# Another order of the score, maximum and value matmuls in an attention step of a fused adaLN block

## The reference, cut to what matters

```python
scores = jnp.einsum('bhqd,bhkd->bhqk', q, k) * scale
scores = jnp.where(causal_mask, -jnp.inf, scores)
attn = jax.nn.softmax(scores, axis=-1)
out = jnp.einsum('bhqk,bhkd->bhqd', attn, v)
```

## Time and profile before

| what | us |
|---|---|
| median of 3 runs | 3058.89 (3057.62 to 3067.77) |
| span of the profiled execution | 3061.1 |
| PE busy | 2843.4 (93%) |
| DVE busy | 2242.9 (73%) |
| ACT busy | 1779.3 (58%) |
| POOL busy | 1253.7 (41%) |
| first to last exponential of attention | 343.1 to 2122.4 |

### The profile page before, as it was taken

One profiled execution on the slowest core, in us unless ns is written; L12 is line 12 of the kernel. 1 busy time (PEld: TensorE's weight loads), 2 busy tenths in 40 slices (PEclk: granted clock), 3 DMA queues, 4 the chain that ended last, 5 costly groups with the idle time before them and its releaser, 6 DMA issues.

```text
span 3061.1 us, 61038 instructions
## 1 busy us (share of the span) xinstructions
PE 2843.4 (93%) x22500; PEld 1573.9 (51%) x22500; DVE 2242.9 (73%) x5047; ACT 1779.3 (58%) x2736; POOL 1253.7 (41%) x1557
## 2 busy tenths in 40 slices
PE   7888799999999999989999999987999999999997
PEld 4433333333433334433333333323888999999997
DVE  7888788888888888899998888822393225566477
ACT  2422466666566665656665566665556666666533
POOL 6766311213521114521114765554305753443176
PEclk9999899999999999999999999998999999999998
DMA  4854323313312322412323535245336765665486
GB/s 163 209 142 106 110 56 65 66 42 76 101 39 56 66 63 59 109 43 37 66 63 91 141 94 123 89 129 152 117 93 204 233 202 175 187 183 173 136 238 193
DMA packets 290690, 359.05 MB, mean 117 GB/s; under 512 B 65404, under 2 KB 243212, under 8 KB 290140
## 3 DMA queue, kind: packets, MB, share of 16 engines
q1 hardware_dynamic: 259516, 279.94, 33.8%
q0 software_dynamic: 26112, 71.34, 7.7%
q10 hardware_dynamic: 4768, 3.88, 0.5%
HBM read 206.25 MB, written 139.21 MB: 113 GB/s over the span
## 4 chain that ended last, share of the span: by engine, by line
PE 49%; ACT 13%; DVE 10%; POOL 7%; issue 7%; DMA 2%; ACTq 1%; POOLq 0%; SPq 0%; DVEq 0%
ACT P L1643 13%; PE PB L1165 10%; PE PB L1092 8%; PE PB L1181 7%; DVE mx L1460 6%; PE PB L1062 6%; PE PB L1039 6%; PE PB L1075 5%; POOL x_slots L1846 4%; PE PB L1106 2%; PE PB L1150 2%; ACTq L1652 1%; POOL yg L1859 1%; PE PB L1129 1%; POOL x_slots L1838 1%
## 5 line engine op out<-in xcount | busy, mean ns | idle before, releaser
L1460 DVE TENSOR_REDUCE mx<-PB 128x1 f32<-128x512 f32 (+3 forms) x2560 | 1406.9, 603 | 214.6 <-PE PB L1039 135.6
L1643 ACT ACTIVATE P<-PB 128x1024 f32<-128x1024 f32 (+3 forms) x1280 | 1095.4, 894 | 643.3 <-PE PB L1075 629.3
L1039 PE MATMUL PB<-KO,QO 64*128 64x512 bf16 (+3 forms) x2560 | 762.0, 353 | 61.5 <-DVE mx L1460 51.5
L1092 PE MATMUL PB<-P,V 128*17 128x512 f32 (+3 forms) x5120 | 599.2, 540 | 11.8 <-POOL P L1797 11.7
L1062 PE MATMUL PB<-QO,KO 64*128 64x512 bf16 (+3 forms) x2560 | 546.8, 353 | 60.0 <-ACT P L1643 33.0
L1039 PEld LDWEIGHTS PB<-KO,QO 64*128 64x128 bf16 x2560 | 203.5, 94 | 718.0 <-DVE mx L1460 533.0
L1075 PE MATMUL PB<-QO,KO 34*128 34x512 bf16 (+3 forms) x2560 | 520.0, 351 | 0.6 <-DMA QO<-nh 0.4
L1797 POOL TENSOR_SCALAR_AFFINE_SELECT P<-P 128x256 f32<-128x256 f32 x512 | 208.6, 414 | 678.8 <-ACT P L1643 673.1
L1165 PE MATMUL PB<-xT,ws 128*128 128x128 f32 x3432 | 433.7, 277 | 7.1 <-ACT xT L1726 7.0
L1165 PEld LDWEIGHTS PB<-xT,ws 128*128 128x128 f32 x3432 | 408.2, 193 | 9.7 <-ACT xT L1726 9.7
L1571 DVE TENSOR_TENSOR haT<-sl,PB 64x128 f32<-64x128 f32 x350 | 101.4, 290 | 411.8 <-ACT sl L1735 407.3
(11 more groups left out here) (178 smaller groups left out, 3218.7 us busy)
## 6 DMA issues: line engine op xcount, KB each, us to landing
xq<-x_slots SPq DMA_DIRECT2D x286, 128.0 KB, 2.8
qk_parts<-pt SPq DMA_DIRECT2D x192, 128.0 KB, 2.4
KO<-qk_parts SPq DMA_DIRECT2D x192, 128.0 KB, 4.1
y_slots<-yo SPq DMA_DIRECT2D x191, 128.0 KB
QO<-qk_parts SPq DMA_DIRECT2D x64, 256.0 KB, 3.4
rden<-rden_rows SPq DMA_DIRECT2D x256, 64.0 KB
y_slots<-mx SPq DMA_DIRECT2D x95, 128.0 KB
v_rows<-vst SPq DMA_DIRECT2D x16, 544.0 KB, 4.0
```

Source lines behind the costliest of these rows:

```text
L1039: mm = pe.matmul(PB[:, bank, 0:n], QO[half, k3, j, 128 * t:128 * t + 128], KO[half, k3, j, 512 * kc:512 * kc + n], start=True, stop=True)
L1092: mm = pe.matmul(PB[32 * j:32 * j + 17, 7, c0:512], V[:, g % 2, kt, 17 * j:17 * j + 17], P[:, pbuf(g, i, j // 2), j % 2, 0:n], start=kt == ...
L1460: dve.tensor_reduce(mx[:, j, t, kc:kc + 1], PB[:, u.bank[item], 0:n], AX.X, ALU.max).then_inc(s["mx"], 1)
L1643: act.activation(P[:, pbuf(g, i, p), :, 0:n], PB[:, 2 * p:2 * p + 2, 0:n], ACT.Exp, scale=0.25).then_inc(s["exp"], 1)
```

## The change

Only the order of the items in a step is changed. `sa(g, i, 3)`, one share of the maxima, `sa(g, i, 2)`, then both `sb` of that pair and `exp(g, i, 1)`; then the next share of the maxima; then heads 1 and 0 of the next step, `sa` and `sb`, with a share of maxima between the two `sb`; then `exp(ahead, 0)`, the last share of the maxima, the values of the step two before, and the pumped work. The number of instructions is the same.

```diff
         ahead = order[n + 1] if n + 1 < len(order) else None
-        if len(pend) == 2:
-            values(*pend.pop(0))
+        o("sa", g, i, 3)
         maxima(at + (quota + 2) // 4)
-        o("sa", g, i, 3)
         o("sa", g, i, 2)
-        maxima(at + quota // 2)
-        if ahead:
-            o("sa", *ahead, 0)
-            o("sa", *ahead, 1)
         o("sb", g, i, 3)
         o("sb", g, i, 2)
         o("exp", g, i, 1)
-        if i >= 2:
-            pumped(pumps)
+        maxima(at + quota // 2)
+        if ahead:
+            o("sa", *ahead, 1)
+        if ahead:
+            o("sa", *ahead, 0)
+        if ahead:
+            o("sb", *ahead, 1)
         maxima(at + quota // 2 + (quota + 2) // 4)
         if ahead:
             o("sb", *ahead, 0)
-            o("sb", *ahead, 1)
-        maxima(at + quota)
         if ahead:
             o("exp", *ahead, 0)
+        maxima(at + quota)
+        if len(pend) == 2:
+            values(*pend.pop(0))
+        if i >= 2:
+            pumped(pumps)
         send_rows()
```

## The result

The changed kernel takes 3270.6 us (median of 4 runs, 3261.2 to 3278.0) against 3061.7 us before (4 runs on the same chip): ratio 1.068, interval 1.066 to 1.070. The profiled execution took 3265.7 us, with a span of 3263.9.

The account below looks back on a forecast made before the run. The prediction took a loop through ACT's exponentials as the bound, then PE. Steps with maxima +333 us, last 44 steps -5, the rest 0: +328 on the 3061.1 span, less 2.2 for the median, gave 3387 us; range 3290 to 3465.

Parts of the forecast that it names:

- The bound before: Full attention step: a loop through ACT, two exponentials at 1.95 plus a 0.72 gap, 2.67 us; PE's own need 2.40.
- The two waits: PE, full step: `sb` 2 waits for `sa` 2 and `sb` 1 for `sa` 1, 0.22 us each, +0.44 together.
- eight instants instead of six (+0.44): PE, full step: fewer neighbouring matmuls in different array halves start together, so two more start instants of 0.22 us.
- the signs that I had named for being wrong: `sb` 2 starting with `sb` 3, H matmuls starting ahead of L ones listed before them, or the clock leaving 1.00.
- rival A: Array halves take work independently, no pairing loss, half the waits filled: about -71 us, 2990 us; chance 0.07.
- The mean step: Attention step at mean width: 3.13 us against 2.57 before, +0.56, bounds +0.46 and +0.70.
- the wider partner of a shared instant: Mean step: two shared instants last as long as the wider matmul when only one is on a diagonal; 0.10 us.
- the main term: Steps with maxima: 595 steps at +0.56 us make +333 us, bounds 274 and 417.
- The last 44 steps: Attention steps without maxima: a full step gains 0.27 us, a narrow one about nothing; -5 us, bounds -12 and +10.
- Everything else in attention: Projections, turns and logits in attention: PE's 117 us exposed, waits for DVE can go; 0 us, bounds -16 to +10.
- B: Rival: pairing lost but the two waits hidden; +0.12 us a step, +71 us, 3130 us; chance 0.11.
- D: Rival: waits set at nothing, on DVE-held banks or projections behind values, add 0.15 us a step; 3480 us; chance 0.05.

Follow-up runs that it names:

- first: Changed kernel with the third maximum of a step listed behind `sb` 0 of the next step instead of ahead of it; ratio 1.059 to the kernel before.
- ninth: Changed kernel with `sb` 0 and `sb` 1 of the next step exchanged around the third maximum; ratio 1.064 to the kernel before.
- twelfth: Changed kernel with heads 0 and 1 of the next step exchanged, in both first and second passes; ratio 1.033 to the kernel before.
- thirteenth: Changed kernel with head numbers exchanged in both pairs, 0 with 1 and 2 with 3; ratio 1.031 to the kernel before.
- fifth: Changed kernel with the first maximum behind `sa` 2 and the second behind the next step's `sa` 1 and 0; ratio 1.010 to the kernel before.
- fourth: Changed kernel with only the first maximum moved, behind `sa` 2, to fill the first wait; ratio 1.034 to the kernel before.
- sixth: Changed kernel with only the second maximum moved, behind the next step's `sa` 1 and 0; ratio 1.033 to the kernel before.
- tenth: Changed kernel with every second pass right behind its own first pass, four unfilled waits a step instead of two; ratio 1.513 to the kernel before.

## Why the prediction was wrong

**The bound before, and the sign: right.** The chain through ACT opened as described: the two exponentials of the step at 672.98 start 1.09 and 2.22 after its first matmul, 1.11 and 2.21 were forecast. ACT's idle time until an `sb` in a group rose from 32.0 to 39.8 us, DVE's from 12.5 to 20.9 (I had said over 30), and PE became the bound nearly everywhere (in the chain over attention DVE's reductions of the maxima are 2.7%, almost all else is PE).

**The two waits: right.** 0.44 from a first pass to its second was forecast; the trace has 0.43 to 0.44 (673.21 to the second `sb` at 673.65; 674.09 to 674.52). I had said that line 1077's weight loads would wait some 1200 times; they did 1287 times in attention. Filling both waits takes 0.40 off a full step (0.44 forecast) and gives back 11.3 of 12.4 us a group.

**The step that failed: "eight instants instead of six (+0.44)", by the rule that start times follow the list.** A matmul may start ahead of ones listed before it if its own half of the array is idle. So `sa` 0 started at 0.68 instead of 1.10 and, what counts, `sb` 0 paired with `sb` 1 and the third maximum with the fourth. That is one instant of 0.22 less, of which 0.05 is lost again ahead of the values (0.35 behind the last pair instead of 0.30): 3.10 instead of 3.27. The term of +0.44 measured +0.26 (3.10 less 2.40 and the two waits of 0.22). One of the signs that I had named for being wrong is there: `sb` 0, in the high half, starts at 674.56, ahead of the low half's maximum at 674.75 listed before it. Of rival A, "the two halves take their work independently", that half was right, and I gave it 0.07 as a whole. My evidence against it, that start times follow the list in every view, was weak and misread. In full steps of the kernel before the halves alternate, and there the two rules give the same starts, so these can't tell them apart. On diagonal steps they can, and the timeline that I used for the earlier trace rows has such a place, at the head of the next step:

```profile
1013.38 0.39 PE L1062 MATMUL PB<-QO,KO 64*128 64x512 bf16 x1
1013.54 0.22 PE L1042 MATMUL PB<-tri,pick 64*128 64x128 bf16 x1
1013.60 0.19 PE L1043 MATMUL PB<-tri,pick 64*128 64x64 bf16 x1
```

The `sa` of head 3, in the high half, starts 0.16 and 0.22 ahead of the two masking matmuls of the low half that are listed before it. So the kernel before already showed the early start.

What rival A lacked is that a weight load whose count isn't reached holds both halves, and that counts come in list order. The first of these is at 674.09 to 674.52: the low half is free and the bank of the third maximum is too, since 674.14 at the latest by its semaphore, yet nothing starts. The first, ninth, twelfth and thirteenth experiments fit these three together, and so does the fifth, which filled the waits.

The Trainium skill's sentence in TensorEngine Tiling (Array Packing), Key Properties, that different tiles can load and multiply in parallel, holds here beyond neighbours. That matmuls stay in program order, as the Trainium skill has it in TensorE: Matmul & The Clock Gate, Step-by-step: what each phase is for, doesn't hold for starts across the two halves (673.66 against 673.87), though it fits the order of the semaphore counts.

**The mean step.** 3.13 was forecast, 2.88 came (115.21 / 40). The full step explains 0.17 of the 0.25. The rest, 0.08, is about the 0.10 that I had put down as an estimate for the wider partner of a shared instant. My reading is that each half works through its own matmuls, so that a wide one in one half doesn't hold up narrow ones in the other; no experiment tests this alone. In line with it are full-width steps with narrow maxima and narrow values, here by their exponentials:

```profile
595.86 2.08 ACT L1645 ACTIVATE P<-PB 128x1024 f32<-128x1024 f32 x2 [0.66 <-PE PB L1077]
598.46 2.14 ACT L1645 ACTIVATE P<-PB 128x1024 f32<-128x1024 f32 x2 [0.52 <-PE PB L1077]
...
600.97 2.09 ACT L1645 ACTIVATE P<-PB 128x1024 f32<-128x1024 f32 x2
```

They are 2.60 and 2.51 apart, below the 2.67 that the same two steps took before: freed from ACT, these steps gain. So the main term is 0.31 x 595 = 184 us instead of 333, outside its bounds of 274 and 417, which were both built on the strict order.

**The small terms.** The last 44 steps: -5 forecast, +4 measured (their 43 intervals from exponential to exponential: 114.8 to 118.4 us). Their full steps did become shorter, 2.48 instead of 2.66, where 2.39 was forecast. But the projections in them were less hidden: a full step with one took 2.91 before (2064.43 to 2067.34) and 3.55 after (2269.41 to 2272.96). And the clock was at half for 24 us instead of 17. Everything else in attention, forecast 0: 206 - 184 - 4 = +18. It is in the first group (125.0 against 106.1 us, 6 more than a clean group's share) and in groups with projections (group 3: 128.0 against 112.8, 3 more). The stretches at the half clock between the first and the last exponential add up to 80 us against 43; if PE's work takes twice as long there, these 37 us hold some 18 us of loss. That is an estimate; the cause of the clock's falls in this kernel wasn't isolated.

**The rivals.** B, waits hidden, fell with the fourth to sixth experiments. D didn't occur. A was wrong as a whole and right in one part. The direction was right for the reason given, mostly: the waits, 0.40 of the 0.43 that a full step lost, were priced rightly, and only the size of the pairing term was off. The range was too narrow because all its terms shared one untested rule.

## What to carry to other kernels

Before moving matmuls in such a list, count two things: how long each half of the array works in a step, and what stands between a matmul and the one that waits for it. Here the second was the price, 0.22 us for each unfilled wait, and filling it with an independent matmul took it away. A rule of order that was read off steps in which the alternatives give the same starts is no evidence. Find a place where they differ, here the diagonal steps of the kernel before, or give the rival a real chance.

## What the runs showed of the hardware that I had not expected

- Starts across the halves: `sa` 0 at 673.66 ahead of the maximum listed two places before it at 673.87, in all 150 steps of full width, and `sa` 3 0.22 us early in the thirteenth kernel.
- Semaphore counts in list order: the second pass came 0.69 us behind its first when a maximum was listed before that first pass but started 0.22 later, 0.44 otherwise. The count of `sa` 3 was 0.03 behind that of the maximum (647.72 and 647.69), though it had started 0.22 ahead.
- A weight load that waits for its count holds both halves: nothing starts from 674.09 to 674.52.
- The clock: four unfilled waits a step brought the mean granted clock in attention from 0.99 to 0.67 and the kernel to 1.51 times the time; the changed kernel with two has 0.98, but so has the fifth with both filled (1825.3 us), so that step from 0.99 can't be put on the waits. In the tenth kernel, waits of a fraction of a microsecond cost more than their sum: a full step of 4.2 us became one of 7.2 for two thirds of the time.
